# Third edge convolution of a fused graph network: the second norm is moved one and two quads behind the first, and TensorE adds the bias

## The chip, the cores and the metric

The kernel runs on one core of a Trainium2 chip. Its engines are PE (TensorE, matrix products into PSUM), PEld (TensorE's loading of weights), DVE (VectorE), ACT (ScalarE), POOL (GpSimd) and SP (SyncE, which issues most DMAs). The metric is the time of one execution in microseconds (us); the median of several executions is compared.

## What is computed

Four small graph networks follow each other: two GCN convolutions, two SAGE convolutions, three edge convolutions and four attention layers, with a layer norm and an addition of earlier features between the networks. Each has 25,000 edges over 50,000 nodes of 128 features. The change lies in the edge convolutions. For layer l of three:

```python
hx = h @ lin_w[l]
ea = relu(edge_attr @ edge_w1[l] + edge_b1[l]) @ edge_w2[l] + edge_b2[l]
msg = hx[row] * w[:, None] + ea
out = segment_sum(msg, col, num_segments=n) + bias[l]
mu = out.mean(-1, keepdims=True)
var = ((out - mu) ** 2).mean(-1, keepdims=True)
h = relu((out - mu) * rsqrt(var + LN_EPS) * ln_w[l] + ln_b[l])
```

After the third layer h is added to an earlier x, and the sum is normed again (the "second norm" here), cut at zero and multiplied with the first attention layer's weights.

## The kernel before

The edges are sorted by target node, cut into 196 tiles of 128 and worked through in 49 quads of four tiles (512 rows), from the last to the first. `KINDS` gives the twelve stages that run one after the other: X, C1, C2, S1, S2, LA, LA, LB, GA, GA, GA, GZ. LA is an edge convolution with its norm, LB the third one with both norms. POOL starts a stage's gathers (line 864) when the whole output of the stage before is stored. Every engine then runs its own program, two quads per turn of its loop, and waits for the others by semaphores; `Steps` counts the named steps (vd: DVE's, ad and ad_t: ACT's, pd: PE's).

In quad n of LA and LB:

- PE (`tile`) sums the messages of quad n+1, tiles 3 to 0: `FS` and `S` are 0/1 selection matrices that DVE writes (`select`, for quad n+2), `CR` and `LO` carry rows over the borders of tiles. `edge_hidden` (eat, ew) and `edge_terms` (ones_row and ew with H1T) make the edge terms of quad n+2; `edge_relu` on ACT lies between them. In LB, `edge_terms` stands at tile 2 and `tail_turn` (transposition of GN) behind it. The sums of a quad lie in PSUM bank 0 or 2.
- DVE adds the bias while it copies the sums into U (line 1349, step "comb"), takes mean and variance (`sums`: BATCH_NORM_STATS2 and AGGREGATE) and the factors (`coef`: rs and nb, from ACT's square root sd), and makes the messages of quad n+2 (line 1264), which need `edge_terms`.
- ACT scales (`scaled`) into GN in LA and into U in LB.
- In LB, `finish_lb` follows on DVE in the same quad: lnw, lnb, x (with XIN, the earlier features), second stats, aggr, rs and nb; ACT scales RB into GN. Only the rest of the tail is behind by one quad (`BEHIND`): PE turns GN (`tail_turn`), ACT copies it to OT, PE multiplies it with WX (`tail_rows`), and ACT copies the rows to RO and NV.
- In LA, PE multiplies OT with linw between the tiles of the next quad (`late_rows`), and ACT writes RO and then OT.

So every quad of LB runs through both norms on DVE before DVE takes up the next. The call that does it:

```python
                    finish(s, kind, n, h, ahead, turn)
                    if more and kind in ("LA", "LB"):
                        messages(s, n + 2, h)
                    if kind == "LB":
                        finish_lb(s, n)
```

Of the kernel before, what the change touches and what calls it, by code (L numbers as in the profile page):

```python
# [21 lines left out]
P = 128  # L22
N = 50000
E = 25000
D = 128
# [3 lines left out]
QUADS = T // 4  # L29
# [14 lines left out]
FIRSTS = CARRY_ROW[3] + 1  # L44
ONE_BANK = ('C1', 'C2', 'S1', 'S2', 'LA', 'LB')
# [51 lines left out]
def gnn_program(nc, a, out):  # L97
# [4 lines left out]
    with ctx:  # L102
# [22 lines left out]
        ones_row = sb("ones_row", [P, P], bf16)  # L125
# [16 lines left out]
        bias_r = sb("bias_r", [P, 3, D])  # L142
# [54 lines left out]
        den = sb("den", [P, 4, 2])  # L197
        ea_in = sb("ea_in", [P, 4, ED])
# [35 lines left out]
        b_in, b_rest, b_sum = (lend(2 * ROOM + 7600 + k * 384, 3, D)[0:3] for k in range(3))  # L234
        b_high, b_mid = (lend(2 * ROOM + 8800 + k * 192, 3, 64)[0:3].bitcast(bf16) for k in (0, 1))
# [3 lines left out]
        e_rest = lend(2 * ROOM + 9300 + 512, 2, 4 * ED)  # L239

# [63 lines left out]
        def steps(name, order, by=1, start=0):  # L304
# [21 lines left out]
            "LA": ("comb", "stats", "aggr", "rs", "nb"),  # L326
            "LB": ("comb", "stats", "aggr", "rs", "nb", "lnw", "lnb", "x", "stats2", "aggr2", "rs2", "nb2"),
# [12 lines left out]
        BEHIND = ("S2", "LB")  # L340
# [101 lines left out]
        loads += [(bias_r[:, l, :], a["L2_gnn_bias"][l].partition_broadcast(P)) for l in range(3)]  # L442
        loads += [(w_in[ED * k:ED * k + ED, :, :], a["L2_gnn_edge_w1"].rearrange("l p c -> p l c")) for k in range(8)]
        loads += [(b_in[:, l, :], a["L2_gnn_edge_b2"][l].partition_broadcast(3)) for l in range(3)]
# [120 lines left out]
        def _(sp):  # L565
# [101 lines left out]
            for s, kind in STAGES[1:]:  # L667
# [10 lines left out]
                def load(n):  # L678
# [7 lines left out]
                    if kind in xin.order:  # L686
                        sp.wait_ge(vd.sem, vd.at(s, n) if first else vd.last(s, n, "x"))
                        sp.dma_start(XIN[:, :, :], quad_rows(X_SRC[s], quad(n))).then_inc(xin.sem, 16)

                def store_x(n):  # L690
                    xstep = {"C2": "x", "S2": "x", "LB": "x"}.get(kind)
                    if xstep:
                        sp.wait_ge(vd.sem, vd.at(s, n, xstep))
                        sp.dma_start(quad_rows(X_DST[s], quad(n)), RB[:, :, :]).then_inc(st_x.sem, 16)
# [13 lines left out]
                if kind == "GZ":  # L708
                    load(0)
                    with sp.Fori(0, LAST) as n:  # L710
                        load(n + 1)
                else:
                    behind = kind in BEHIND + LATE

# [24 lines left out]
        def _(pool):  # L739
# [5 lines left out]
            g.memset(ones_row[:, :], 1.0).then_inc(c_pool, 1)  # L745
            pool.wait_ge(c_pool, 4)
            g.affine_select(out=ident[:, :], in_=ident[:, :], compare_op=ALU.not_equal, fill=1.0, base=0,
# [175 lines left out]
        def _(dve):  # L923
# [79 lines left out]
            for in_, rest, sum_, high, mid, mask, to in (  # L1003
                    (w_in, w_rest, w_sum, w_high, w_mid, is_part, ew1[:, :, :]),
                    (b_in, b_rest, b_sum, b_high, b_mid, ident[0:3, 0:3], None)):
# [18 lines left out]
            link(v.tensor_scalar(c2_r[:, :], bias_r[:, 2, :], mv[:, 0, 0:1], rs[:, 0:1], ALU.subtract, ALU.mult))  # L1024
# [207 lines left out]
            def select(s, n, h, j):  # L1232
# [16 lines left out]
                to = S[:, 4 * h + j, :]  # L1249
                if weight is None:  # L1250
# [42 lines left out]
            def finish(s, kind, n, h, ahead, turn=0):  # L1293
# [90 lines left out]
            def finish_lb(s, n):  # L1384

                dve.wait_ge(ad.sem, ad.at(s, n, "n"))
# [694 lines left out]
```

## Time and profile before

| | |
|---|---|
| median of 3 runs | 6893.03 us (6882.67 to 6896.57) |
| the profiled execution: its time | 6876.37 us |
| its span, first to last instruction | 6874.6 us |
| mean granted TensorE clock | 0.840 of 2.4 GHz |
| busy share: PE, PEld, DVE, ACT, POOL | 66%, 55%, 56%, 43%, 52% |
| stages LA, LA, LB (first to last line 1349) | 3486 to 3767, 3790 to 4070, 4094 to 4632 us |

The shares are means over twelve stages that run one after the other; what a change in one stage does is read from that stage's own rows.

### The profile page before, as it was taken

The numbers are of one execution on the slowest core, as the hardware profiler recorded it, in microseconds if no ns is written. First come the engines' busy times: TensorE is split into PE (matmuls) and PEld (weight loads), VectorE is DVE, ScalarE is ACT, GpSimd is POOL, SyncE is SP. The second block draws the span as 40 slices with busy tenths as digits, with TensorE's granted clock in tenths as the row PEclk, the third lists the DMA queues.
The fourth block names the chain that finished last, engine by engine and source line by source line (L and its number), as shares of the span: only waits on it lengthen the run. The fifth ranks groups of instructions, "written<-read, shape, count | busy, mean of one in ns | idle before, by whom it ended". The sixth has DMA issues, their size and how long they took to land. (4 is left out here: it accounts for less than half of the span.)

```text
span 6874.6 us, 127291 instructions
## 1 busy us (share of the span) xinstructions
PE 4515.9 (66%) x28875; PEld 3780.7 (55%) x28950; DVE 3833.9 (56%) x13851; ACT 2953.7 (43%) x7261; POOL 3552.3 (52%) x4582
## 2 busy tenths in 40 slices
PE   4888888888878767887789986660281282183065
PEld 2666666666656666666778876660271172072064
DVE  5666666766654487335777777770360261162176
ACT  3666666666633233334567765550130031031043
POOL 3434343444457174714655757106556556656666
PEclk9899999999999966998899998875695596596566
DMA  2555444445444275535743334322232132132133
GB/s 81 158 162 160 164 166 165 163 171 173 163 127 116 80 202 166 141 103 157 216 122 101 114 99 134 93 81 55 55 105 62 49 104 69 44 104 76 46 109 91
DMA packets 1002697, 815.63 MB, mean 119 GB/s; under 512 B 103820, under 2 KB 836818, under 8 KB 1002616
## 3 DMA queue, kind: packets, MB, share of 16 engines
q1 hardware_dynamic: 908536, 650.27, 30.8%
q0 software_dynamic: 94080, 164.48, 9.3%
q8 instruction: 26, 0.43, 0.0%
q14 instruction: 55, 0.45, 0.0%
HBM read 359.28 MB, written 459.01 MB: 119 GB/s over the span
## 5 line engine op out<-in xcount | busy, mean ns | idle before, releaser
L864 POOL DMA_INDIRECT G<-table,idx_all x1568 | 1525.4, 973 | 1284.9 <-issue 669.2
L1435 PE MATMUL PS<-G,S 128*128 (+2 forms) x4312 | 857.6, 306 | 5.8 <-DMA G<-table,idx_all 1.7
L1435 PEld LDWEIGHTS PS<-G,S 128*128 128x128 f32 x4312 | 733.8, 221 | 56.5 <-issue 48.1
L864 POOL DMA_INDIRECT G<-table,idx_l x588 | 583.2, 992 | 338.7 <-issue 178.3
L1758 ACT ACTIVATE CR<-PS 65x128 f32<-65x128 f32 (+3 forms) x1078 | 289.2, 268 | 1017.2 <-PE PS L1435 1005.6
L1435 PE MATMUL PS<-CR,LO 97*128 97x128 f32 (+1 forms) x4312 | 658.7, 302 | 64.6 <-ACT CR L1758 64.6
L1432 PE MATMUL PS<-ident,ES 128*98 128x128 f32 x16 | 4.2, 421 | 1003.5 <-DVE ES L475 1003.5
L1435 PE MATMUL PS<-G,FS 128*65 (+2 forms) x3234 | 514.2, 299 | 215.0 <-DVE den L1367 100.6
L1435 PEld LDWEIGHTS PS<-CR,LO 97*128 97x128 f32 x4312 | 610.8, 218 | 77.3 <-ACT CR L1758 77.3
L475 DVE COPY ES<-G 128x392 f32<-128x392 f32 x4 | 2.1, 527 | 1018.0 <-DMA G<-table,idx_all 1018.0
L1432 PEld LDWEIGHTS PS<-ident,ES 128*98 128x98 f32 x16 | 2.6, 191 | 1004.7 <-issue 1004.6
L1435 PEld LDWEIGHTS PS<-G,FS 128*65 128x65 f32 x3234 | 391.4, 150 | 278.9 <-issue 256.2
L1435 PE MATMUL PS<-w,H1T 128*128 128x128 f32 x2352 | 358.5, 311 | 224.8 <-DVE H1T L1099 193.8
L1758 ACT ACTIVATE G<-G 128x128 f32<-128x128 f32 x1176 | 483.0, 482 | 13.9 <-DVE G L1085 0.6
L1758 ACT ACTIVATE W<-V 98x1024 f32<-98x1024 f32 x4 | 4.2, 1056 | 1093.1 <-DVE V L517 1093.1
L1435 PEld LDWEIGHTS PS<-w,H1T 128*128 128x128 f32 x2352 | 325.9, 219 | 252.1 <-issue 214.7
L1138 DVE COPY G<-PS 128x520 f32<-128x520 f32 x392 | 271.2, 692 | 281.9 <-DMA table<-G 179.5
L1240 DVE TENSOR_TENSOR LO<-iota_row,relK 128x512 f32<-128x512 f32 x539 | 406.4, 754 | 0.1
L1251 DVE TENSOR_SCALAR S<-iota_row,rel 128x128 f32<-128x128 f32 x1372 | 380.7, 281 | 0.4 <-PE PS L1435 0.4
L1435 PEld LDWEIGHTS PS<-WX,G 128*128 128x128 f32 x2352 | 290.4, 191 | 160.2 <-issue 160.1
L886 POOL TENSOR_TENSOR OWN<-OWN,PT 128x256 f32<-128x256 f32 x294 | 175.7, 619 | 325.0 <-DMA OWN<-table 325.0
L1435 PE MATMUL PS<-WX,G 128*128 128x130 f32 x2352 | 321.6, 280 | 27.5 <-DVE G L1138 23.6
(292 smaller groups left out, 11284.0 us busy)
## 6 DMA issues: line engine op xcount, KB each, us to landing
table<-G SPq DMA_DIRECT2D x392, 260.0 KB, 2.7
table<-G SPq DMA_DIRECT2D x392, 256.0 KB, 2.6
table<-RO SPq DMA_DIRECT2D x245, 256.0 KB
table<-RO SPq DMA_DIRECT2D x196, 260.0 KB
OWN<-table SPq DMA_DIRECT2D x196, 260.0 KB
XIN<-xrows SPq DMA_DIRECT2D x196, 256.0 KB
OWN<-table SPq DMA_DIRECT2D x147, 256.0 KB
xrows<-RB SPq DMA_DIRECT2D x147, 256.0 KB
```

The costliest lines, as they stand in the source:

```text
L475: v.tensor_copy(ES[:, :, :], G[:, :, D:GW].rearrange("p t h -> p h t")).then_inc(m_v.sem, 1)
L864: g.indirect_dma_start(G[:, t, 0:w], None, TAB[s], bass.IndirectOffsetOnAxis(ap=idx[:, t:t + 1], axis=0)).then_inc(gat[t % 4].sem, 16)
L886: last = g.tensor_tensor(oh, oh, wide(PT[:, 2 + h, ds(Q4, 4)], 64), ALU.mult)
L1138: done(q, 3, v.tensor_copy(PR[t], pair(6)))
L1240: v.tensor_tensor(LO[:, 4 * h:4 * h + 4, :], iota_row[:, :].unsqueeze(1).to_broadcast([P, 4, P]), wide(relK[:, ds(Q4, 4)], P), ALU.is_equal)
L1251: i = v.tensor_scalar(to, iota_row[:, :], rel[:, ds(Q4 + j, 1)], None, ALU.is_equal)
L1432: return nc.tensor.transpose(o, i, ident[0:k, 0:k])
L1435: return nc.tensor.matmul(o, l, r, start=start, stop=stop)
L1758: return nc.scalar.activation(o, i, fn, **kw)
```

## The change

In LA and LB, TensorE adds the bias: one bf16 matrix product (`ones_bias` with `eb2`, whose rows 32 to 34 now hold the bias in three bf16 pieces) opens the PSUM bank of each quad, `ones_row` is masked to the rows below 32, and the prologue cuts the bias as it did the edge bias. DVE takes its stats from PSUM and ACT scales from PSUM, so the addition of line 1349 is gone; the bank is free again when ACT has scaled ("n"), where before it was free after "comb".

In LB the first norm of quad n now runs with lnw, lnb, x and the second stats of quad n-1, and with the second factors and second scaling of quad n-2. The second norm has its own stat2, mv2, sd2, rs2 and nb2 and its own counts (vd2, vd3, ad2), and the scaled rows alternate between U and OWN (`LBU`). The four selections S of a quad are one instruction. On PE all four tiles of quad n+1 come first, then `tail_turn` of n-2, then `edge_terms` of n+2, then `tail_rows` of n-2. DVE runs two more turns at the end. The other stages keep their order; PE's and ACT's loops start at quad 3 everywhere, with quads 1 and 2 written out.

The core of the diff:

```diff
+        LBU = (U[:, :, :], OWN[:, :, 0:D])
...
+        vd2 = steps("vd2", {"LB": ("lnw", "lnb", "x", "stats", "aggr")})
+        vd3 = steps("vd3", {"LB": ("rs", "nb")})
+        ad2 = steps("ad2", {"LB": ("sd", "g")})
+        BEHIND = {"S2": 1, "LB": 2}
...
+        loads += [(b_in[BIAS:BIAS + 3, l, :], a["L2_gnn_bias"][l].partition_broadcast(3)) for l in range(3)]
...
+                elif kind == "LB":
+
+                    def turn(n):
+                        at = n if isinstance(n, int) else 2
+                        if at < LAST - 2:
+                            load_attr(n + 3)
+                        if at > 0:
+                            load(n)
+                            store_x(n - 1)
+                        if at > 1:
+                            store(n - 2)
...
+            for in_, rest, sum_, high, mid, mask, to, row in (
+                    (w_in, w_rest, w_sum, w_high, w_mid, is_part, ew1[:, :, :], 0),
+                    *[(b_in[r:r + 3], b_rest[r:r + 3], b_sum[r:r + 3], b_high[r:r + 3], b_mid[r:r + 3],
+                       ident[r:r + 3, r:r + 3], None, r) for r in (0, BIAS)]):
...
+                if KINDS[s] == "LB":
+                    if j == 2:
+                        v.tensor_tensor(S[:, 4 * h:4 * h + 4, :], iota_row[:, :].unsqueeze(1).to_broadcast([P, 4, P]),
+                                        wide(rel[:, ds(Q4, 4)], P), ALU.is_equal).then_inc(sel.sem, 4)
+                    return
...
-                elif kind in ("LA", "LB"):
-                    if kind == "LA":
-                        dve.wait_ge(ad.sem, ad.last(s, n, "n"))
+                elif kind == "LA":
                     aggregated(s, n)
-                    step(s, n, v.tensor_tensor(U4, A, on4(bias_r[:, s - 5, :]), ALU.add), "comb", s3)
-                    sums(s, n, U, "", (s2,), (s1,))
+                    sums(s, n, A, "", (s3, s2), (s1,))
                     coef(s, n, "", (s0,))
...
+            def finish_lb(s, n, h, ahead):
+
+                s3, s2, s1, s0 = ahead
+                x_, sums_ = LBU[1 - h], bank(2 * h)
+                now = not isinstance(n, int) or n <= LAST
+                late = not isinstance(n, int) or 0 < n <= LAST + 1
+                later = not isinstance(n, int) or n > 1
+                if now:
+                    aggregated(s, n)
+                    for j in range(4):
+                        i = v.bn_stats(stat[:, j, :], sums_[:, j, :])
+                    i.then_inc(vd.sem, 1)
+                if later:
+                    dve.wait_ge(ad2.sem, ad2.at(s, n - 2, "sd"))
+                    v.reciprocal(rs2[:, :], sd2[:, :]).then_inc(vd3.sem, 1)
+                if late:
+                    dve.wait_ge(ad.sem, ad.at(s, n - 1, "n"))
+                    lnw = step2(s, n - 1, v.tensor_tensor(x_, x_, on4(lnw_r[:, :]), ALU.mult), "lnw")
+                if later:
+                    alone(dve, (vd3.sem, vd3.at(s, n - 2, "rs")))
+                    v.scalar_tensor_tensor(nb2[:, :], mv2[:, :, 0], -1.0, rs2[:, :], ALU.mult,
+                                           ALU.mult).then_inc(vd3.sem, 1)
+                if now:
+                    alone(dve, (vd.sem, vd.at(s, n, "stats")))
+                    for j in range(4):
+                        i = v.bn_aggr(mv[:, j, :], stat[:, j, :])
+                    i.then_inc(vd.sem, 1)
+                s3()
+                if late:
+                    lnw()
+                    lnb = step2(s, n - 1, v.tensor_tensor(x_, x_, on4(lnb_r[:, :]), ALU.add), "lnb")
+                if now:
+                    dve.wait_ge(ad.sem, ad.at(s, n, "sd"))
+                    v.reciprocal(rs[:, :], sd[:, :]).then_inc(vd.sem, 1)
+                s2()
+                if now:
+                    alone(dve, (vd.sem, vd.at(s, n, "rs")))
+                    v.scalar_tensor_tensor(nb[:, :], mv[:, :, 0], -1.0, rs[:, :], ALU.mult, ALU.mult).then_inc(vd.sem, 1)
+                if late:
+                    dve.wait_ge(xin.sem, xin.at(s, n - 1, "rows"))
+                    dve.wait_ge(st_x.sem, st_x.at(s, n - 1))
+                    dve.wait_ge(ad2.sem, ad2.last(s, n - 1, "g"))
+                    lnb()
+                    x_made = step2(s, n - 1, v.scalar_tensor_tensor(RB[:, :, :], x_, 0.0, XIN[:, :, :],
+                                                                    ALU.max, ALU.add), "x")
+                if not isinstance(n, int) or n < LAST - 1:
+                    messages(s, n + 2, h)
+                if late:
+                    x_made()
+                    for j in range(4):
+                        i = v.bn_stats(stat2[:, j, :], RB[:, j, :])
+                    step2(s, n - 1, i, "stats")()
+                    for j in range(4):
+                        i = v.bn_aggr(mv2[:, j, :], stat2[:, j, :])
+                    i.then_inc(vd2.sem, 1)
...
-                    pe.wait_ge(vd.sem, vd.at(s, n, "comb") - 2 * len(vd.order[kind]))
+                    if kind in ("LA", "LB"):
+                        pe.wait_ge(ad.sem, ad.at(s, n, "n") - 2 * len(ad.order[kind]))
+                        mm(PS[:, 2 * h, :], ones_bias[:, :], eb2[:, s - 5, :, :].rearrange("p j c -> p (j c)"),
+                           True, False)
+                    else:
+                        pe.wait_ge(vd.sem, vd.at(s, n, "comb") - 2 * len(vd.order[kind]))
...
-                            if j == (2 if kind == "LB" else 1) and edge and at < LAST - 1:
+                            if j == (0 if kind == "LB" else 2) and at >= behind:
+                                tail_turn(s, n - behind)
+                            if j == (0 if kind == "LB" else 1) and edge and at < LAST - 1:
                                 edge_terms(s, n + 2)
-                            if j == 2 and kind in BEHIND and at:
-                                tail_turn(s, n - 1)
-                            if j == 0 and kind in BEHIND and at:
-                                tail_rows(s, n - 1)
+                            if j == 0 and at >= behind:
+                                tail_rows(s, n - behind)
...
-                    scaled(s, n, ACT.Identity, "", U)
+                    scaled(s, n, ACT.Identity, bank(2 * h))
...
                 elif kind == "LB":
-                    ahead(3)
+                    at = n if isinstance(n, int) else 2
+                    if at < LAST:
+                        carried(s, n + 1, 1 - h, 3)
                     sqrts(s, n)
-                    scaled(s, n, ACT.Identity, "", U, U)
-                    ahead(2, 1, 0)
-                    sqrts(s, n, "2")
-                    scaled(s, n, ACT.Relu, "2")
+                    if at > 1:
+                        scaled2(s, n - 2)
+                    if at < LAST - 1:
+                        edge_relu(s, n + 2)
+                    if at > 1:
+                        tail_turned(s, n - 2)
+                    scaled(s, n, ACT.Identity, bank(2 * h), LBU[h])
+                    if at < LAST:
+                        carried(s, n + 1, 1 - h, 0)
+                    if at:
+                        sqrts2(s, n - 1)
+                    if at > 1:
+                        tail_out(s, n - 2)
```

`step2` issues a step counted in vd2 and returns its wait; `sqrts2` and `scaled2` are ACT's square root and scaling with the second set of buffers.

Where instructions stand now, in LB. DVE (waits in brackets; G<-G,wl,PS are the messages), the last part of a quad behind the loop, before:

```order
L1264 SCALAR_TENSOR_TENSOR G<-G,wl,PS 128x128 [waits gat3,pd_e]
L1264 SCALAR_TENSOR_TENSOR G<-G,wl,PS 128x128 [waits gat2]
L1264 SCALAR_TENSOR_TENSOR G<-G,wl,PS 128x128 [waits gat1]
L1264 SCALAR_TENSOR_TENSOR G<-G,wl,PS 128x128 [waits gat0]
L1387 TENSOR_TENSOR U<-U,lnw_r 128x512 [waits ad]
L1388 TENSOR_TENSOR U<-U,lnb_r 128x512 [waits vd,c_pool]
L1392 SCALAR_TENSOR_TENSOR RB<-U,XIN 128x512 [waits st_x,xin,ad,vd,c_pool]
L1276 BN_STATS stat<-RB 128x6 [waits vd,c_pool]
L1276 BN_STATS stat<-RB 128x6 x3
L1279 BN_AGGR mv<-stat 128x2 [waits vd,c_pool]
L1279 BN_AGGR mv<-stat 128x2 x3
L1286 RECIPROCAL rs<-sd 128x4 [waits ad]
```

and after:

```order
L1465 RECIPROCAL rs<-sd 128x4 [waits ad]
L1293 TENSOR_TENSOR S<-iota_row,rel 128x512 [waits agg]
L1469 SCALAR_TENSOR_TENSOR nb<-mv,rs 128x4 [waits vd,c_pool]
L1475 SCALAR_TENSOR_TENSOR RB<-OWN,XIN 128x512 [waits c_pool,ad2,vd2,st_x,xin]
L1310 SCALAR_TENSOR_TENSOR G<-G,wl,PS 128x128 [waits gat3,pd_e]
L1310 SCALAR_TENSOR_TENSOR G<-G,wl,PS 128x128 [waits gat2]
L1310 SCALAR_TENSOR_TENSOR G<-G,wl,PS 128x128 [waits gat1]
L1310 SCALAR_TENSOR_TENSOR G<-G,wl,PS 128x128 [waits gat0]
L1482 BN_STATS stat<-RB 128x6 [waits vd2,c_pool]
L1482 BN_STATS stat<-RB 128x6 x3
L1485 BN_AGGR mv<-stat 128x2 [waits vd2,c_pool]
L1485 BN_AGGR mv<-stat 128x2 x3
```

x (RB<-) stands ahead of the messages, of the quad before; rs and nb of the second norm are no longer at the end.

ACT, one quad ahead of the loop, before:

```order
L1758 ACTIVATE CR<-PS 65x128 [waits rsum]
L1758 ACTIVATE CR<-PS 1x128 [waits agg]
L1758 ACTIVATE CR<-PS 65x128 [waits rsum]
L1758 ACTIVATE H1T<-PS,eb 128x512 [waits pd_e]
L1758 ACTIVATE sd<-mv,eps 128x4 [waits vd]
L1758 ACTIVATE U<-U,nb,rs 128x128 [waits vd]
L1758 ACTIVATE U<-U,nb,rs 128x128 x3
L1758 ACTIVATE CR<-PS 1x128 [waits agg]
L1758 ACTIVATE sd<-mv,eps 128x4 [waits vd]
L1758 ACTIVATE GN<-RB,nb,rs 128x128 [waits vd]
L1758 ACTIVATE GN<-RB,nb,rs 128x128 x3
```

and after:

```order
L1864 ACTIVATE CR<-PS 65x128 [waits rsum]
L1864 ACTIVATE sd<-mv,eps 128x4 [waits vd]
L1864 ACTIVATE GN<-RB,nb,rs 128x128 [waits vd3]
L1864 ACTIVATE GN<-RB,nb,rs 128x128 x3
L1864 ACTIVATE H1T<-PS,eb 128x512 [waits pd_e]
L1864 ACTIVATE OT<-PS 128x512 [waits pd]
L1864 ACTIVATE U<-PS,nb,rs 128x128 [waits vd]
L1864 ACTIVATE U<-PS,nb,rs 128x128 x3
L1864 ACTIVATE CR<-PS 1x128 [waits agg]
L1864 ACTIVATE sd<-mv,eps 128x4 [waits vd2]
L1864 ACTIVATE RO<-PS 128x520 [waits pd,st_t]
L1864 ACTIVATE NV<-PS 128x4x4
```

The scaling GN<-RB now stands ahead of H1T, and waits for vd3 of two quads before; sd of the first norm stands ahead of it.

PE, one quad ahead of the loop, before (PS<-eb,ones_row and PS<-ew,H1T are `edge_terms`):

```order
L1435 MATMUL PS<-G,FS 65x128 [waits mprod,sel,vd]
L1435 MATMUL PS<-G,FS 65x128 [waits mprod] x2
L1435 MATMUL PS<-G,S 128x128 [waits mprod]
L1435 MATMUL PS<-eat,ew 128x512 [waits eas]
L1435 MATMUL PS<-G,S 128x128 [waits mprod,sel]
L1435 MATMUL PS<-eb,ones_row 128x512 [waits mprod,ad_e]
L1435 MATMUL PS<-ew,H1T 128x128 x4
L1435 MATMUL PS<-G,S 128x128 [waits mprod,sel] x2
L1435 MATMUL PS<-CR,LO 128x128 [waits carry]
L1435 MATMUL PS<-CR,LO 128x128 x3
```

and after:

```order
L1531 MATMUL PS<-eb,ones_bias 128x512 [waits ad]
L1531 MATMUL PS<-G,FS 65x128 [waits mprod,sel]
L1531 MATMUL PS<-G,FS 65x128 [waits mprod] x2
L1531 MATMUL PS<-G,S 128x128 [waits mprod]
L1531 MATMUL PS<-eat,ew 128x512 [waits eas]
L1531 MATMUL PS<-G,S 128x128 [waits mprod,sel] x3
L1531 MATMUL PS<-CR,LO 128x128 [waits carry]
L1531 MATMUL PS<-CR,LO 128x128 x3
L1528 MATMUL PS<-ident,GN 128x128 [waits ad_t,ad2]
L1528 MATMUL PS<-ident,GN 128x128 x3
L1531 MATMUL PS<-eb,ones_row 128x512 [waits mprod,ad_e]
L1531 MATMUL PS<-ew,H1T 128x128 x4
```

The product with ones_bias is new, and `edge_terms` has moved from behind tile 3's sums to behind the transposition of GN.

## Rows read from the trace of the kernel before

**Rows 1.** Windows of LA and LB: busy us of PE, PEld, DVE, ACT, POOL; clock; DMA.
```profile
3500.00:3760.00 260.00, 250.05 (x1938) 225.42 (x1961) 204.15 (x941) 194.85 (x446) 174.33 (x176) 1.00 0.39 112
...
4100.00:4330.00 230.00, 143.61 (x871) 138.35 (x880) 168.10 (x697) 121.03 (x323) 176.29 (x176) 0.80 0.47 132
4345.00:4625.00 280.00, 177.01 (x1081) 170.63 (x1092) 202.34 (x840) 148.41 (x397) 0.00 (x0) 0.80 0.29 81
```

**Rows 2.** The bias addition of line 1349, in the first LA stage and in LB.
```profile
L1349 DVE TENSOR_TENSOR U<-PS,bias_r x49: 684/692/693, 3486.4 to 3766.6; 128x512 f32<-128x512 f32 x49
...
L1349 DVE TENSOR_TENSOR U<-PS,bias_r x49: 683/692/693, 4094.0 to 4632.2; 128x512 f32<-128x512 f32 x49
```

**Rows 3.** Timeline of one LB quad: start us, us, engine, line, operation, idle before.
```profile
4343.28 0.61 PE L1435 MATMUL PS<-eb,ones_row 128*128 128x512 bf16 x1 [4.73 <-ACT H1T L1758]
...
4343.68 1.92 PE L1435 MATMUL PS<-ew,H1T 128*128 128x128 f32 x8
...
4345.87 1.12 DVE L1264 SCALAR_TENSOR_TENSOR G<-G,wl,PS 128x128 f32 x4 [1.60 <-PE PS L1435]
...
4346.91 0.69 DVE L1387 TENSOR_TENSOR U<-U,lnw_r 128x512 f32<-128x512 f32 x1
...
4349.57 0.87 DVE L1276 BATCH_NORM_STATS2 stat<-RB 128x6 f32<-128x128 f32 x4
...
4350.55 0.38 DVE L1279 BATCH_NORM_AGGREGATE mv<-stat 128x2 f32<-128x6 f32 x4
...
4350.97 0.30 ACT L1758 ACTIVATE sd<-mv,eps 128x4 f32<-128x4 f32 x1 [1.77 <-DVE mv L1279]
...
4351.59 0.16 DVE L1287 SCALAR_TENSOR_TENSOR nb<-mv,rs 128x4 f32<-128x4 f32 x1
4351.78 1.65 ACT L1758 ACTIVATE GN<-RB,nb,rs 128x128 f32<-128x128 f32 x4 [0.52 <-DVE nb L1287]
4351.82 0.69 DVE L1349 TENSOR_TENSOR U<-PS,bias_r 128x512 f32<-128x512 f32 x1
...
4353.09 0.28 DVE L1251 TENSOR_SCALAR S<-iota_row,rel 128x128 f32<-128x128 f32 x1
```

**Rows 4.** Timeline of one quad of the first LA stage.
```profile
3706.01 0.39 PE L1435 MATMUL PS<-eb,ones_row 128*128 128x512 bf16 x1
...
3706.23 1.05 PE L1435 MATMUL PS<-ew,H1T 128*128 128x128 f32 x8
...
3707.56 1.12 DVE L1264 SCALAR_TENSOR_TENSOR G<-G,wl,PS 128x128 f32 x4 [0.78 <-PE PS L1435]
...
3708.51 0.65 PE L1432 MATMUL PS<-ident,GN 128*128 128x128 f32 x4
...
3708.95 0.60 ACT L1758 ACTIVATE RO<-PS 128x512 f32<-128x512 f32 x1
...
3709.44 0.77 ACT L1758 ACTIVATE OT<-PS,lnb_c,lnw_c 128x512 f32<-128x512 f32 x1
...
3710.27 0.49 PE L1435 MATMUL PS<-linw,OT 128*128 128x128 f32 x2 [0.23 <-ACT OT L1758]
...
3711.01 0.69 ACT L1758 ACTIVATE H1T<-PS,eb 128x512 f32<-128x512 f32 x1 [0.64 <-remote]
```

**Rows 5.** Who waited for OT in the first LA stage: us, times.
```profile
  PE PS L1435: 5.1, 23
```

**Rows 6.** Timeline of the prologue: DVE cuts the three-partition weights into pieces.
```profile
58.84 0.35 DVE L1006 CAST G<-G 3x384 bf16<-3x384 f32 x1
...
62.49 1.92 DVE L1017 CAST eb<-G 3x384 bf16<-3x384 f32 x4
```

**Rows 7.** Timeline of the end of LB and the start of the next stage.
```profile
4632.22 0.69 DVE L1349 TENSOR_TENSOR U<-PS,bias_r 128x512 f32<-128x512 f32 x1
...
4645.70 1.09 PE L1432 MATMUL PS<-ident,GN 128*128 128x128 f32 x4 [7.13 <-ACT NV L1758]
...
4653.31 0.95 POOL L864 DMA_INDIRECT G<-table,idx_all  x1 [314.59 <-DMA table<-RO]
```

More of the change, by code:

```diff
@@ L124, in gnn_program @@
         eps = sb("eps", [P, 1])
-        ones_row = sb("ones_row", [P, P], bf16)
+        ones_row, ones_bias = (sb(n, [P, P], bf16) for n in ("ones_row", "ones_bias"))
         w1 = sb("w1", [P, 256])
@@ L325, in gnn_program @@
             "S2": ("comb", "x", "stats", "aggr", "rs", "nb"),
-            "LA": ("comb", "stats", "aggr", "rs", "nb"),
-            "LB": ("comb", "stats", "aggr", "rs", "nb", "lnw", "lnb", "x", "stats2", "aggr2", "rs2", "nb2"),
+            "LA": ("stats", "aggr", "rs", "nb"),
+            "LB": ("stats", "aggr", "rs", "nb"),
             "GA": ("den", "comb", "dene", "rden", "norm"),
@@ L711, in _ @@
                         load(n + 1)
+                elif kind == "LB":
[8 more added lines that the diff above has]
+                            store(n - 2)
+                    for n in (0, 1, 2):
+                        load_attr(n)
+                    load(0)
+                    turn(0)
+                    turn(1)
+                    with sp.Fori(2, LAST - 2) as n:
+                        turn(n)
+                    for n in (LAST - 2, LAST - 1, LAST):
+                        turn(n)
+                    store_x(LAST)
+                    store(LAST - 1)
+                    store(LAST)
                 else:
-                    behind = kind in BEHIND + LATE
+                    behind = kind in BEHIND or kind in LATE
                     def turn(n):
@@ L1382, in finish, with step2 @@
                         v.tensor_tensor(OUTR[h][:, :, 0:D], U[:, :, :], XIN[:, :, :], ALU.add).then_inc(vd.sem, 1)
[L1384 to L1394 removed]
+            def step2(s, n, ins, name):
+                ins.then_inc(vd2.sem, 1)
+                return lambda: alone(dve, (vd2.sem, vd2.at(s, n, name)))
@@ L1733, in quad @@
                     if kind in BEHIND and at == LAST:
[L1734 to L1736 removed]
+                        tail_rows(s, n - behind)
+                        for k in range(n - behind + 1, n + 1):
+                            tail_turn(s, k)
+                            tail_rows(s, k)
                 if kind in ("LA", "LB"):
@@ L1747, in _ @@
                 quad(0, 0)
-                with pe.Fori(0, LAST // 2 - 1) as m:
+                quad(1, 1)
+                quad(2, 0)
+                with pe.Fori(1, LAST // 2 - 1) as m:
                     quad(m * 2 + 1, 1)
@@ L2049, in _ @@
                 quad(0, 0)
-                with act.Fori(0, LAST // 2 - 1) as m:
+                quad(1, 1)
+                quad(2, 0)
+                with act.Fori(1, LAST // 2 - 1) as m:
                     quad(m * 2 + 1, 1)
```

101 lines of the change are left out of this document (59 added, 42 removed), and 1 row of the table ad.

## The prediction

> **What bounds the kernel now.** I read the windows by stage first. In LA, PE is busy 250 of 260 us at the full granted clock; in LB no engine is: PE 177 of 280 us, DVE 202, ACT 148, at a mean clock of 0.80 [rows 1]. So LB is bound by a ring of waits. The bias addition stands once in each quad: its first and last start give periods of 280.2/48 = 5.84 us in LA and 538.2/48 = 11.21 us in LB [rows 2].
>
> The timeline of one LB quad shows the ring. DVE waits 1.60 us for the edge terms and makes the messages; then lnw, lnb, x, stats, aggr, ACT's square root, rs, nb, and ACT's scaling of 1.65 us. Only behind that scaling comes H1T on ACT, for which PE has then stood idle 4.73 us, and only then the edge terms of the next quad [rows 3]. POOL's gathers do not lengthen it: LB has them in its first part (176 of 230 us busy) and not in its second, and the DVE share (73% and 72%) and the clock are the same [rows 1].
>
> LA has another ring, of PE and ACT alone: the turned sums, RO, OT, PE's product of OT with linw, eat, H1T, edge terms, the border products, and again RO. PE waits for OT where that product starts (0.23 us in the quad shown), in 23 of 45 quads and 5.1 us in all [rows 4, 5].
>
> **LB, the new ring.** Durations at the upper of TensorE's two levels (2.4 GHz), counted from the start of the first stats of quad n:
>
> - DVE: stats 0.87, rs of n-2 taken as nb's 0.16, lnw 0.69, nb 0.16, aggr 0.38: 2.3 us [rows 3].
> - ACT: sd of n 0.30, then the second scaling of n-2, 1.65, which stands behind sd on ACT: 4.2 us [rows 3].
> - PE: the transposition 0.65: 4.9; H1T (0.69) runs beside it on ACT. Then `edge_terms`, from 3706.01 to 3707.28, 1.27: 6.15 us [rows 4].
> - DVE: 0.28 until the messages start (3707.28 to 3707.56), 1.04 until the next instruction can start (4345.87 to 4346.91): 7.5 us [rows 3, 4]. Before them DVE has LO, S, lnb, rs, nb and x to do, three 512-wide operations more of about 0.69 with LO, FS and the wide S; that ends at about 5.5, inside the wait. The bias addition and S in four parts (0.28 each) are gone from DVE, but this saves nothing here, since DVE waits for the edge terms anyway.
> - DVE: second stats to aggr 0.98, aggr 0.38, and 0.23 to the next quad (nb to the next addition) [rows 3]: 9.1 us.
>
> So T = 9.1 us with PE at its upper level. At the lower level (1.2 GHz) `edge_terms` took 4343.28 to 4345.60, 2.32 us, 1.05 more [rows 3], and the transposition 1.09, 0.44 more [rows 7]: T = 10.6. A mean clock of 0.80 means that four tenths of the time are at the lower level [rows 1]. I keep this share: PE still idles twice in a quad, about 2 us ahead of the transposition (border products done at about 2, scaling at 4.2) and some 0.5 us ahead of the border products. T = 9.1 + 0.4 x 1.5 = 9.7 us. LB then gains 48 x (11.21 - 9.7) = **72 us**.
>
> What leaves the path is covered: ACT's first scaling of n runs from about 5.5 to 7.1 and DVE wants it at 1.1 of the next quad, after 10 us; PE sums quad n+1 two thirds of a quad ahead of need. XIN is now loaded in SP's queue after x of the quad before (at 5.5) and wanted a whole period later; store_x and the table's store behind it on SP have the same room. Nothing on SP waits for something that is later than before by more than a quad.
>
> **Reading PSUM.** No row has stats or a scaled copy of 128 columns from PSUM. Below, nothing: the addition took 0.692 us from PSUM and lnw 0.69 from SBUF [rows 2, 3]. Above, for ACT: OT, scaled from PSUM, took 0.77 for 512 columns [rows 4]; four at that price are 3.1 instead of 1.65. In LB that is still off the ring; in LA the missing addition (0.69) covers half of the 1.4, and 0.7 x 96 = 67 us would be left. I take nothing, since the addition's row is nearest. For DVE the upper end is as much again per read, 0.87 more, 42 us in LB; I take nothing.
> The Trainium skill (VectorE: DVE Perf Modes, section on the TRN2 errata) speaks against this change: it gives VectorE a fixed 120 cycles for a source in PSUM and 58 in SBUF, ScalarE 172 and 224. Four stats would pay 0.26 us more on the ring, an estimate from that page, 12 us over LB; the sum would end at 6847 instead of 6835. The rows of the addition do not show it.
>
> **LA.** The new product is 512 columns in bf16. The one with ones_row holds PE for 0.22 us before the next starts (3706.01 to 3706.23) [rows 4]. It stands ahead of the wait for OT, which covers it in the 23 of 45 quads that wait 0.22 us on average [rows 5]. In the others nothing covers it but the register work of a loop turn. From both sides: 0, and 0.22 x 96 = 21 us. I take 0.15 in every second quad: **+7 us**. The addition that DVE loses is not in LA's ring, so LA gains nothing inside; its last quad, serial to the store, is 0.69 shorter in each of two stages: -1.4 us. The new wait for ACT's "n" costs nothing, since PE has already waited for the same scaling before it transposes. Behind it FS, S and eat are queued, for which H1T waits.
>
> **Prologue and drain.** DVE's cutting into pieces on three partitions runs serially from 58.84 to 64.41 [rows 6] and is now done twice: **+5.6 us**. From the last addition to the first gather of the next stage are 21.1 us [rows 7]. Now the second norm of the last two quads is left over, one after the other on ACT and PE: 1.65 + 1.09 + 0.7 for scaling, turning and copying once more, **+3.5 us** (bounds 0 and 7).
>
> **Sum.** -72 + 7 - 1.4 + 5.6 + 3.5 = -58 us. The profiled execution took 6876 and would take 6818; the median of the runs shown is 17 us higher, 6893, so the forecast is **6835 us**.
>
> **Rivals.**
> - The clock stays up. PE's idle piece falls from 4.73 us to about 2; the clock was at its full level through LA, where PE hardly idles [rows 1]. Then T = 9.1, gain 101, sum -86: 6807. For it: every idle piece is less than half as long. Against it: 2 us of 9 are still idle in one piece. Chance 0.27. The Trainium skill (TensorE: Matmul & The Clock Gate, "What's actually happening") has the clock fall when the array has been idle and return after sustained work; by it this rival's time holds.
> - The lower level falls on the ring each time, because the idle piece lies just ahead of the transposition and the edge terms: T = 10.6, gain 29, sum -14: 6879. For it: before, the edge terms behind the idle piece were at the lower level in the quad shown [rows 3]. Chance 0.17.
> - The ring is shorter than I think (the scaling on ACT gets ahead) and DVE alone bounds LB: its work by the same rows is about 7.9 us, with gaps 8.3. Gain 140: 6768. For it: DVE's idle is only 1 us a quad in my ring. Chance 0.06.
> - Slower. PE becomes LB's bound at the lower level: busy 0.63 x 11.2 = 7.1 us a quad at a clock of 0.80 is about 5.6 us of work at the upper one, with the bias 5.8, at the lower one 11.6. If the level stays low, T is 11.6 and more, +19 in LB and +15 elsewhere: 6927 or above. It decides from T = 10.9 on, where LB's gain equals the other terms. Against it: a PE that works without idling was at the full clock in LA [rows 1]. Chance 0.05.
>
> My forecast, T from 9.4 to 10.3, has 0.45. About 0.2% (14 us) is what a measurement can tell from no change. Faster by more: below 6879, all of the first and third rival, the forecast and half of the second: 0.86; within: 0.09; slower: 0.05. The range, 8 times in 10, goes from 6790 (the clock rival with an LA that costs nothing) to 6880 (the second rival).
>
> **What would show it.** Line 1442's stats should start every 9.7 us in LB; DVE should wait about 1 us for the edge terms ahead of the messages; `edge_terms` should start right behind the transposition of GN, and that right behind the scaling from RB; the clock in LB should be 0.80 or more. LA should keep 5.84 to 5.95 us with PE at the full clock. The prediction is wrong if the clock in LB differs much from 0.80, if scaling from PSUM takes much over 1.65 us, or if LA's period moves by more than 0.2 us.

## The result and the profile after

The changed kernel takes **6792.2 us** (median of 4 runs, 6787.6 to 6795.7); the kernel before, timed beside it, 6894.8 us (4 runs). The ratio is 0.9853, with a 95% interval of 0.9836 to 0.9870: some 102 us gained. In a later session it was 6789.6 against 6880.8, a ratio of 0.9864 (0.9848 to 0.9879), or 91 us. The changed kernel's two medians lie 3 us apart; the kernel before had medians of 6881 to 6882 in three later sessions (33 runs), 13 us under the first four runs, so 91 is the surer figure. The forecast was 6835 us, a gain of 58.

The stages show where it went. Each length runs from the first gather of a stage to that of the next; before and after were each profiled twice.

| us | to the first gather | S2 | LA, 1st | LA, 2nd | LB | three GA stages | whole span |
|---|---|---|---|---|---|---|---|
| before | 1970.7, 1971.4 | 316.6, 317.0 | 303.7, 302.4 | 303.9, 303.8 | 570.8, 572.4 | 1606.2, 1613.0 | 6874.6, 6883.6 |
| after | 1979.3, 1982.3 | 319.6, 317.8 | 300.1, 300.3 | 299.9, 300.4 | 470.7, 469.7 | 1619.1, 1615.1 | 6793.0, 6791.6 |

Stages left out differ by under 2 us. LB gives 101 us, the two LA stages 6, the beginning takes back 10, and the GA stages differ as much between two profiles of one kernel (7 us) as between the two kernels.

The windows of LA and LB after the change (columns as in [rows 1]):

```profile
3512.00:3772.00 260.00, 248.88 (x1960) 231.61 (x2004) 177.24 (x891) 181.11 (x446) 175.56 (x178) 1.00 0.40 112
...
4110.00:4330.00 220.00, 164.51 (x1040) 147.95 (x1062) 163.01 (x717) 133.53 (x376) 169.71 (x166) 0.87 0.54 148
4345.00:4530.00 185.00, 137.34 (x884) 123.12 (x901) 137.31 (x603) 115.13 (x325) 2.99 (x3) 0.88 0.37 102
```

LA is the same stage as before: PE is busy 249 of 260 us at the full clock. In LB PE is busy 75% of the time instead of 63%, and the clock rose from 0.80 to 0.87. The first statistics of LB, once a quad:

```profile
L1442 DVE BATCH_NORM_STATS2 stat<-PS x196: 266/281/300, 4099.6 to 4534.5; 128x6 f32<-128x128 f32 x196
```

The last quad's four begin at 4533.92 (below), so the period is 434.3/48 = **9.05 us**, where [rows 2] gave 11.21 and the forecast 9.7. One whole turn of the new ring, from the timeline of the changed kernel, with PE at its upper level:

```profile
4399.33 0.89 DVE L1442 BATCH_NORM_STATS2 stat<-PS 128x6 f32<-128x128 f32 x4
...
4400.22 0.66 DVE L1449 TENSOR_TENSOR U<-U,lnw_r 128x512 f32<-128x512 f32 x1
...
4400.87 0.38 DVE L1457 BATCH_NORM_AGGREGATE mv<-stat 128x2 f32<-128x6 f32 x4
...
4401.28 0.30 ACT L1864 ACTIVATE sd<-mv,eps 128x4 f32<-128x4 f32 x1 [0.82 <-DVE mv L1457]
4401.48 1.63 ACT L1864 ACTIVATE GN<-RB,nb,rs 128x128 f32<-128x128 f32 x4
...
4403.02 0.67 ACT L1864 ACTIVATE H1T<-PS,eb 128x512 f32<-128x512 f32 x1
...
4403.25 0.66 PE L1528 MATMUL PS<-ident,GN 128*128 128x128 f32 x4 [1.57 <-ACT GN L1864]
...
4403.82 0.39 PE L1531 MATMUL PS<-eb,ones_row 128*128 128x512 bf16 x1
...
4404.04 1.05 PE L1531 MATMUL PS<-ew,H1T 128*128 128x128 f32 x8
...
4404.44 1.50 ACT L1864 ACTIVATE OWN<-PS,nb,rs 128x128 f32<-128x128 f32 x4
...
4405.40 1.12 DVE L1310 SCALAR_TENSOR_TENSOR G<-G,wl,PS 128x128 f32 x4 [1.33 <-PE PS L1531]
...
4406.44 0.87 DVE L1482 BATCH_NORM_STATS2 stat<-RB 128x6 f32<-128x128 f32 x4
...
4407.41 0.38 DVE L1485 BATCH_NORM_AGGREGATE mv<-stat 128x2 f32<-128x6 f32 x4
...
4408.09 0.89 DVE L1442 BATCH_NORM_STATS2 stat<-PS 128x6 f32<-128x128 f32 x4 [0.30 <-issue]
```

The steps are those of the forecast: 8.76 us from 4399.33 to 4408.09. The [0.30] of issue in front of the last row comes in every second quad. In a kernel whose PE stays at the upper level (the filler run below) the statistics start 8.76 and 8.38 us apart in turn, so that I take 8.57 on average for this ring. The next quad of the same timeline has PE at its lower level. There the ring took until 4417.86, 9.77 us, for these rows:

```profile
4412.00 1.11 PE L1528 MATMUL PS<-ident,GN 128*128 128x128 f32 x4 [1.95 <-ACT GN L1864]
...
4413.33 1.91 PE L1531 MATMUL PS<-ew,H1T 128*128 128x128 f32 x8 [0.22 <-issue]
```

Who waits in 4110 to 4330 is in the groups (busy us, mean ns of one | idle before):

```profile
L1310 DVE SCALAR_TENSOR_TENSOR G<-G,wl,PS 128x128 f32 x92 | 25.8, 344 | 47.7 <-PE PS L1531 47.7
...
L1528 PE MATMUL PS<-ident,GN 128*128 128x128 f32 x96 | 18.6, 325 | 42.3 <-ACT GN L1864 42.3
```

That is 23 or 24 quads: DVE waits 2.0 us in each for the edge terms, and PE 1.8 us for the scaling. Before, PE's idle piece was 4.73 us, in front of the edge terms [rows 3]. The prologue and the end of LB, where the forecast had two small costs:

```profile
64.49 0.35 DVE L1047 CAST G<-G 3x384 bf16<-3x384 f32 x1
...
68.15 1.92 DVE L1058 CAST eb<-G 3x384 bf16<-3x384 f32 x4
70.11 0.29 DVE L1060 BATCH_NORM_STATS2 stat<-bias_r 128x6 f32<-128x128 f32 x1
...
4533.92 0.89 DVE L1442 BATCH_NORM_STATS2 stat<-PS 128x6 f32<-128x128 f32 x4 [1.25 <-ACT CR L1864]
...
4558.36 0.94 POOL L904 DMA_INDIRECT G<-table,idx_all  x1 [209.76 <-DMA table<-RO]
```

The second cut takes 70.11 - 64.49 = 5.6 us. From the last start to the next stage's gather are 24.4 us, where it was 21.1 [rows 7].

### The profile page after: what moved, and what is told of

Same layout as the page of the kernel before. It is cut to its first block and busy times, and to the rows that moved or that the text cites. A ratio compares the mean times of both kernels' runs of the same rounds, so it can differ in the third digit from the quotient of the medians.

```text
span 6793.0 us, 126255 instructions
## 1 busy us (share of the span) xinstructions
PE 4495.4 (66%) x28956; PEld 3757.9 (55%) x29097; DVE 3721.0 (55%) x13568; ACT 2906.8 (43%) x7261; POOL 3556.3 (52%) x4585
## 5 line engine op out<-in xcount | busy, mean ns | idle before, releaser
L1531 PE MATMUL PS<-G,S 128*128 (+2 forms) x4312 | 829.5, 300 | 5.1 <-DMA G<-table,idx_all 1.5
L1531 PEld LDWEIGHTS PS<-G,S 128*128 128x128 f32 x4312 | 710.0, 215 | 54.8 <-issue 46.8
L1531 PE MATMUL PS<-CR,LO 97*128 97x128 f32 (+1 forms) x4312 | 635.9, 295 | 83.7 <-ACT CR L1864 83.4
L1531 PEld LDWEIGHTS PS<-CR,LO 97*128 97x128 f32 x4312 | 581.9, 209 | 103.0 <-ACT CR L1864 103.0
```

The costliest lines, as they stand in the source:

```text
L1531: return nc.tensor.matmul(o, l, r, start=start, stop=stop)
```

## The experiments

The theory: LB's period is a ring that runs once round DVE, ACT and PE (first statistics, second scaling, transposition, edge terms, messages, second statistics); what lies on it costs in full, what lies in DVE's wait in front of the messages costs nothing, and PE's lower clock level costs about 0.6 us a quad. The rivals: DVE's own busy time sets the period; the gain is the missing addition and not the order; the clock can't be had back by the kernel. Each median is told beside the one of the kernel before in the same session: 6881.8 for the first four runs, 6881.8 for the next four, 6880.8 for the last four. Their spread makes differences under some 8 us between sessions mean little, so that the length of LB in the profile is given each time.

**The two halves of the change.** First TensorE's bias alone, in the kernel before:

```diff
-step(s, n, v.tensor_tensor(U4, A, on4(bias_r[:, s - 5, :]), ALU.add), "comb", s3)   # DVE, LA and LB
+mm(PS[:, 2 * h, :], ones_bias[:, :], eb2[:, s - 5, :, :].rearrange("p j c -> p (j c)"), True, False)   # PE
```

> The kernel before, with TensorE's bias in LA and LB and without the change of LB's order: the first and second norms of LB stay one behind the other as before. If nearly all of LB's gain (100 us) is the new order, this LB stays within 0.44+1.1 us a quad of the period before (11.2 us), that is gains 20 to 55 us by the addition of 0.7 to 1.1 us that no longer stands in the chain, and LA gives 4 us back as in the changed kernel: 6835 to 6870. If the prediction's 'gone from DVE saves nothing' holds, LB gains under 5 us: 6885 to 6892. If the GA stages' +4 us each (three stages, +13 in all) come with the bias constants and not with the order, they are here too; otherwise GA is as before.

Measured: 6881.9, a ratio of 0.9998 (0.9989 to 1.0007). LB 568.4, LA 298.9 and 299.9. The bias taken from DVE is worth 3 us in LB in the old order and 8 in the two LA stages; the beginning is 8 longer in this profile. The timeline of this kernel shows why it does nothing in LB:

```profile
4355.34 0.16 DVE L1295 SCALAR_TENSOR_TENSOR nb<-mv,rs 128x4 f32<-128x4 f32 x1
4355.53 1.65 ACT L1768 ACTIVATE GN<-RB,nb,rs 128x128 f32<-128x128 f32 x4 [0.52 <-DVE nb L1295]
4355.56 0.89 DVE L1284 BATCH_NORM_STATS2 stat<-PS 128x6 f32<-128x128 f32 x4
```

In the old order the next quad's first norm starts on DVE together with ACT's 1.65 us of scaling, as the addition did in [rows 3]; it is in that scaling's shadow. Then the new order alone, DVE adding in LA and LB:

```diff
+v.tensor_tensor(LBU[h], sums_, on4(bias_r[:, :]), ALU.add)      # ahead of the first statistics
-v.bn_stats(stat[:, j, :], sums_[:, j, :])
+v.bn_stats(stat[:, j, :], LBU[h][:, j, :])
```

> The other half of the change alone: LB in the new order with its own buffers, and DVE adding the bias in LA and in LB as before (in LB directly ahead of the first statistics, which then read the sum). If the chain statistics, second scaling, transposition, edge terms, messages sets the period, the addition and the wait for it stand in it: LB comes out near the 516 us of the run with one DVE operation more at that place, 510 to 530, LA at 304, the whole at 6835 to 6845. If the addition is as free in the new order as it was in the old one, LB is 471 to 475 and the whole 6790 to 6800.

Measured: 6833.1, ratio 0.9927 (0.9914 to 0.9941), LB 518.2, LA 303.9 and 301.9. From this kernel's timeline:

```profile
4407.75 0.38 DVE L1492 BATCH_NORM_AGGREGATE mv<-stat 128x2 f32<-128x6 f32 x4
4408.06 0.69 DVE L1445 TENSOR_TENSOR OWN<-PS,bias_r 128x512 f32<-128x512 f32 x1
...
4408.85 0.87 DVE L1452 BATCH_NORM_STATS2 stat<-OWN 128x6 f32<-128x128 f32 x4
```

Here the addition stands on the ring: 0.79 us from its start to that of the statistics. So LB is 571.6 before (mean of two), 568.4 with the bias alone, 518.2 with the order alone, 470.2 with both. The halves give 3 and 53 apart, and 101 together: the bias is worth 48 us behind the order, 1.0 us a quad. 0.79 of it is the ring; the rest goes with the clock, 0.83 and 0.84 in the two windows here and 0.87 and 0.88 with both halves.

**One DVE operation more, at two places of the changed kernel.**

```diff
+v.tensor_tensor(spare[:, :, :], sums_, on4(lnw_r[:, :]), ALU.add)             # a: ahead of the first statistics
+v.tensor_tensor(spare[:, :, :], on4(lnb_r[:, :]), on4(lnw_r[:, :]), ALU.add)  # b: ahead of the messages
```

> The changed kernel, with one DVE addition of 4x128 columns from PSUM more (its output isn't used), put directly ahead of the first statistics in LB, where before the bias addition stood. If the ring from statistics to messages and back sets the period, the 0.7 us comes in full each quad: 49 x 0.7 = +34, 6826 (a part may be given back by or lost to the clock: +25 to +50). If DVE's wait in front of the messages takes it up, +0 to 5: 6792 to 6797.

> The changed kernel, with the same kind of DVE addition of 4x128 columns more (from SBUF, its output isn't used), but directly ahead of LB's messages, where DVE waits 1.3 us or more for the edge terms. If the ring sets the period, the wait takes it up: 6792 to 6800. If DVE's busy time sets it, +0.7 x 49 = +34: 6826.

Measured, a: 6830.6, ratio 0.9919, LB 515.6: +45 us, 0.93 a quad. b: 6781.2, ratio 0.9856 (0.9841 to 0.9871), LB 472.1: +2. The waits of the messages in b:

```profile
L1311 DVE SCALAR_TENSOR_TENSOR G<-G,wl,PS 128x128 f32 x96 | 26.9, 343 | 34.5 <-PE PS L1534 33.8 <-DMA G<-table,idx_l 0.7
```

That is 1.44 us a quad, and 2.07 in the changed kernel (47.7 in 23 quads): the wait took in 0.6 of the operation's 0.68 us. The same kind of operation costs 45 us at one place and 2 at the other, 4.65 us further in the same quad (4401.47 and 4406.12 in b's timeline). That rules out DVE's busy time as the bound. In a the statistics start 0.61 us behind the operation (4405.03 and 4405.64); the rest of the 0.93 goes with the clock, which was 0.84 and 0.83 in the two windows.

**S in four parts**, as before the change:

```diff
-v.tensor_tensor(S[:, 4 * h:4 * h + 4, :], iota_row[:, :].unsqueeze(1).to_broadcast([P, 4, P]),
-                wide(rel[:, ds(Q4, 4)], P), ALU.is_equal)
+for k in (3, 2, 1, 0):
+    v.tensor_scalar(S[:, 4 * h + k, :], iota_row[:, :], rel[:, ds(Q4 + k, 1)], None, ALU.is_equal)
```

> The changed kernel, with LB's selections built by four instructions in place of one (0.44 us more of DVE a quad). In the changed LB, DVE waits 1.3 to 2.7 us in front of the messages, after S: if that wait absorbs it, the time stays at 6792 (within 5). If DVE's busy time sets the period, it rises by 0.44 x 49 = 21: 6813.

Measured: 6785.1, ratio 0.9854, LB 469.1. It costs nothing. The operation was smaller than I wrote: the four took 21.7 us in 24 quads and the one 15.8, 0.25 us a quad, so that a DVE bound would have cost 12 us and not 21.

**LA's bias by DVE**, the rest as changed:

> The changed kernel, with LA's bias added by DVE as before; LB is left as changed. If LA's -3.7 and -4.0 us are the added bias gone from the start and the end of each LA stage, both LA stages go back to 303.7: 6800, +8 against the changed kernel. If they are something else that the change brought, LA stays at 300 and the time at 6792.

Measured: LA 304.0 and 303.8, LB 470.6, whole 6789.1. By the profile LA's 4 us a stage are TensorE's bias (in nine kernels with it LA took 298.7 to 300.7, in those without 301.9 to 304.0); in the whole time 8 us are no more than the spread.

**The clock.** Six matmuls of 128 columns more in each quad, into a bank that nobody reads, ahead of the transposition:

```diff
 def tail_turn(s, n):
+    if KINDS[s] == "LB":
+        for j in range(6):
+            mm(PS[:, 3, 0:P], ident[:, :], iota_row[:, :])
```

> The changed kernel, with six matmuls of 128 columns more in each quad of LB, ahead of the transposition, into a bank that nobody reads (work that the result doesn't need). If the lower granted clock (0.87 to 0.88 in LB) comes from TensorE's waits and costs a quad at the lower level about 1 us in the ring, the granted clock goes to 1.0 and the period to 8.8: LB gains 15 to 25 us: 6767 to 6777. If the matmuls cost as much as they give: 6790 to 6810, clock higher. If the clock isn't theirs to hold, clock as before and 6792 or more.

Measured: 6749.7, ratio 0.9808 (0.9794 to 0.9821), LB 436.6, a larger gain than I expected. Its windows, its first statistics, and three of them in a row (the view ends behind the first instruction of the last):

```profile
4110.00:4330.00 220.00, 193.78 (x1465) 166.27 (x1464) 175.33 (x768) 146.74 (x412) 169.41 (x167) 1.00 0.56 156
4345.00:4490.00 145.00, 128.02 (x968) 109.82 (x967) 116.10 (x510) 96.19 (x273) 0.00 (x0) 1.00 0.38 107
...
L1442 DVE BATCH_NORM_STATS2 stat<-PS x196: 265/281/300, 4096.2 to 4500.8; 128x6 f32<-128x128 f32 x196
...
4382.84 0.89 DVE L1442 BATCH_NORM_STATS2 stat<-PS 128x6 f32<-128x128 f32 x4 [0.30 <-issue]
...
4391.21 0.89 DVE L1442 BATCH_NORM_STATS2 stat<-PS 128x6 f32<-128x128 f32 x4
...
4399.97 0.30 DVE L1442 BATCH_NORM_STATS2 stat<-PS 128x6 f32<-128x128 f32 x1 [0.30 <-issue]
```

PE idles less, the clock is full, and the period is 404.6/48 = 8.4 us (the row's last start is up to 0.6 behind the first of its four; from first to first it is 4500.23 - 4096.24, 8.42 us a quad) for 9.05. So the lower level cost the changed kernel 0.63 us in each quad, 30 us, and LB is 34 shorter in all: the end of the stage, from the last start to the next gather, is 3 shorter too (21.0 us for 24.4). This run answers the clock rival: with the clock up, T is 8.4 and not 9.1.

**The ring broken.** First PE does the edge terms ahead of the transposition; in the second kernel ACT also does the relu ahead of the square root and the scaling:

```diff
 # PE, at tile 0
-tail_turn(s, n - behind); edge_terms(s, n + 2)
+edge_terms(s, n + 2); tail_turn(s, n - behind)
 # ACT, second kernel only
-sqrts(s, n); scaled2(s, n - 2); edge_relu(s, n + 2)
+edge_relu(s, n + 2); sqrts(s, n); scaled2(s, n - 2)
```

> The changed kernel, with TensorE doing LB's edge terms of the next quad ahead of the transposition of the quad behind. If TensorE's order puts transposition (0.66 us) into the ring between the scaling and the edge terms, taking it out shortens each quad by up to 0.66 us less what else then comes last; the relu on ScalarE for those terms (behind the scaling there) still holds them, so the gain is 0 to 0.6 us a quad: 6763 to 6792, and I take 6775. If the ring goes another way than through the transposition, 6792.

> As the last, and ScalarE does the relu for the next quad's edge terms ahead of the square root and the scaling of the quad behind, so that the edge terms wait for neither. If the ring statistics, scaling, relu, edge terms, messages is what sets the period, it is broken here and DVE's own busy time (7.4 us a quad of the windows and some 0.7 of gaps) sets it: 8.0 to 8.3 us for 8.75 to 10, LB gains 35 to 60 us: 6732 to 6757. If the period is set by something else (TensorE at the lower clock, or the waits on transfers), 6780 to 6792.

Measured, the first: 6760.2, ratio 0.9820 (0.9807 to 0.9834), LB 448.8. The 21 us in LB lie in the 0 to 29 that I expected, and the reason was wrong. From its timeline:

```profile
4299.94 1.63 ACT L1866 ACTIVATE GN<-RB,nb,rs 128x128 f32<-128x128 f32 x4
...
4301.47 0.67 ACT L1866 ACTIVATE H1T<-PS,eb 128x512 f32<-128x512 f32 x1
...
4302.27 0.39 PE L1531 MATMUL PS<-eb,ones_row 128*128 128x512 bf16 x1 [1.78 <-ACT H1T L1866]
```

From the start of the scaling to the product with ones_row are 2.33 us; in the changed kernel they were 2.34 (4401.48 to 4403.82). At the upper level ACT's relu takes as long as PE's transposition beside it, so nothing came off the ring. What came is the clock: 0.96 and 0.98 in the two windows of LB, for 0.87 and 0.88, and the products with H1T take over 1.5 us in 2 of 49 quads, where in the changed kernel they did in 28.

The second: **6690.2, ratio 0.9719** (0.9706 to 0.9733), LB 382.0, the fastest kernel here, some 100 us under the changed one, 88 of them in LB. Its windows, its first statistics and three groups of 4110 to 4330:

```profile
4110.00:4330.00 220.00, 185.41 (x1356) 155.99 (x1355) 204.10 (x907) 175.48 (x483) 169.59 (x166) 0.99 0.64 176
4345.00:4430.00 85.00, 72.13 (x534) 60.89 (x532) 79.44 (x351) 68.82 (x188) 0.00 (x0) 1.00 0.44 124
...
L1442 DVE BATCH_NORM_STATS2 stat<-PS x196: 278/281/301, 4091.5 to 4438.1; 128x6 f32<-128x128 f32 x196
...
L1310 DVE SCALAR_TENSOR_TENSOR G<-G,wl,PS 128x128 f32 x120 | 33.4, 338 | 0.0
...
L1475 DVE SCALAR_TENSOR_TENSOR RB<-U,XIN 128x512 f32<-128x512 f32 x15 | 11.2, 747 | 5.8 <-ACT GN L1866 5.8
L1475 DVE SCALAR_TENSOR_TENSOR RB<-OWN,XIN 128x512 f32<-128x512 f32 x15 | 10.4, 693 | 2.2
```

The period is 7.2 us, and DVE is busy 93% of it. My 8.0 to 8.3 was too long because 7.4 us a quad of busy time was misread: DVE's windows in the changed kernel give 163.01 x 9.05/220 = 6.7, and here 204.10 x 7.2/220 = 6.7 again. The wait in front of the messages is gone; 8.0 us in 30 quads remain in front of x, which overwrites RB and waits until ACT's second scaling has read it. Whether DVE now is the bound was asked with S in four parts in this kernel:

> The kernel with relu and edge terms ahead of the second norm's scaling and transposition, with LB's selections built by four instructions in place of one (0.44 us more of DVE a quad). In the changed kernel the same edit cost nothing. If DVE's busy time is what sets LB's period now, it costs 0.44 x 49 = 21 us: 6711 against 6690. If another wait still sets it: 6690 to 6695.

Measured: 6691.6, ratio 0.9729, LB 383.2, +1 us. DVE was busy 4.4 us more in the window (208.49), and the idle time in front of x fell by 4.3:

```profile
L1476 DVE SCALAR_TENSOR_TENSOR RB<-U,XIN 128x512 f32<-128x512 f32 x15 | 10.5, 702 | 3.7 <-issue 2.6 <-ACT GN L1867 1.0
L1476 DVE SCALAR_TENSOR_TENSOR RB<-OWN,XIN 128x512 f32<-128x512 f32 x15 | 10.2, 680 | 0.0
```

The edit added little to DVE's work (the four selections took 27.5 us in 30 quads, the one 19.8, 0.26 a quad and not 0.44), and the wait in front of x took most of it. So the bound was not yet DVE alone, as I had expected; by these rows it is a second ring through RB and ACT's scaling that is about as long. No run shortened that ring, so that this is argued from the waits and not shown.

**Both kernels once more**, for the spread between executions:

> The kernel before, once more, for a second profile: whether the GA stages' 535 us and the first stage's 1971 us are its own (then 534 to 536 and 1970 to 1972 again, and the +4 and +9 of the changed kernel are the change's), or differ from one execution to the next by as much (then 535 to 540 and 1970 to 1980).

> The changed kernel once more, beside the two above on one chip: 6785 to 6795 and a ratio of 0.985 to 0.987; LB 470 to 472 us, LA 300. If the first stage and the GA stages vary between executions, this profile shows them elsewhere than 1979 and 540.

They are the second numbers of the table above. LB, LA and the time to the first gather came out within 3 us of the first profile; the GA stages of before did not (538.4, 537.8, 536.8 for 534.7, 535.7, 535.8), so no cost there can be put down to the change. The time to the first gather is less sure than two profiles make it look: ten more kernels with the second cut had 1970.4 to 1979.2, the lowest of them under that of the kernel before.

## Why the forecast was right in kind and short in size

- **What bounded LB**: right. A ring of waits, now shown by the same kind of operation costing 45 us on it and 2 us in its wait.
- **The steps of the new ring**: right, each in its place. Their sum at the upper level, 9.1 us, was too long; it measured 8.57. The step that failed is "stats 0.87, rs 0.16, lnw 0.69, nb 0.16", 1.88 us, which took 1.54 (4399.33 to 4400.87): the durations of rows were added, but each DVE instruction starts up to 0.1 us before the one ahead of it ends. sd to scaling was 0.20 for 0.30, the transposition 0.57 (4403.25 to 4403.82) for 0.65, the scaling to the transposition 1.77 for 1.65, and the way back to the next statistics 0.68 or 0.30 for 0.61; 0.06 is rounding upwards in the forecast's sum. Together 0.5 us a quad, 25 us. Starts should be subtracted, as the forecast did elsewhere.
- **The clock's term**, 0.4 x 1.5 = 0.6 us a quad: right in its product, measured 0.63 by the filler. Its parts were not: the clock rose to 0.87, so that a quarter of the time is at the lower level and not four tenths, but those stretches fall on PE's part of the ring more often than that: in the trace of the changed kernel the products with H1T take over 1.5 us in 28 of 49 quads (1.05 at the upper level) and the transposition over 0.9 in 16. So the second rival, by which the lower level falls on the ring each time, had part of the truth; its 10.6 us a quad did not come. The rival "the clock stays up" did not come true. Its 6807 is nearer to the result than 6835 only because it shares the ring that was too long; with the clock up, the result is 6750.
- **LB in sum**: the 48 periods gave 104 us for 72. Of the 32, 25 are the sum of the ring at the upper level, and some 7 are the first and last quads, which are shorter than the steady ones (8.42 us over all 48 periods of the filler run, 8.57 steady); the clock's 0.03 us more a quad takes 1 back. The stage as a whole gave 101, since its end is 3 us longer, which the forecast had as a term of its own.
- **"This saves nothing here"**, of the bias addition and of S in four parts: right for S (-1 us), wrong for the addition. DVE's wait absorbs only what stands between the statistics and the messages; the addition would stand ahead of the statistics, on the ring, for 48 us. The sum did not suffer, since its ring began at the statistics, but the reason given for the addition is wrong: DVE's wait could not have taken it in. That the bias alone gave 3 us in the old order has another cause, the shadow of ACT's scaling.
- **Reading PSUM**: priced at nothing, near enough. Four stats took 0.89 from PSUM and 0.87 from SBUF (0.89 against 0.87 in the rows above); ACT's scaling took 1.50 from PSUM (4404.44) and 1.63 from SBUF (4401.48). The Trainium skill (VectorE: DVE Perf Modes, section on the TRN2 errata), from whose cycles the forecast estimated 0.26 us more for four stats from PSUM, is not borne out: the rows differ by 0.02 us. For ScalarE, where it gives PSUM the lower cost, the rows agree in direction.
- **LA**: +7 - 1.4 was forecast, -6 to -7 came. The term of 0.15 us for the bias product in every second quad fails: the period in the middle of the stage is 5.83 us before and after, so the product is covered in all quads. The addition was gone from the start of the stage as well as from its end: the first statistics of the first LA stage start 11.5 us behind the first gather, for 13.0.
- **Prologue and drain**: 5.6 us as forecast, in each kernel; how much of it reaches the end is less sure (the stage's end scatters by 9 us). Drain 24.4 - 21.1 = 3.3 for 3.5.
- **The slower rival**, PE as LB's bound at the lower level: no trace of it. PE is busy 75% of the time. **The rival with DVE alone as the bound** did not come true either, since DVE waits 2.0 us a quad for the edge terms; its 8.3 us were too high besides, as the kernel with the ring broken runs at 7.2.
- **The signs it named**: the order of the instructions and LA's period are as it said. The clock in LB was 0.87 and not 0.80, and DVE's wait 2.0 us and not about 1 (1.33 with PE at its upper level).
- **The whole**: 58 forecast, 32 more from LB's periods and 12 more from LA make 102, the difference of the first medians. That this is also the first session's figure is partly luck: the two pairs of profiles are 82 and 92 us apart, because the beginning and the GA stages, which scatter by as much, took more back than the 5.6 us forecast.

## What to carry to other kernels

Draw the ring that sets the period, and price each edit by where it stands on it: an operation of 0.69 us cost 45 us at one place and 2 at another, and an edit that is worth nothing in one order (3 us) can be worth 48 once another edit has changed what it stands in. Two halves of a change can't be judged one at a time. Then look who waits in the ring for someone who merely stands ahead in a queue: moving the edge terms in front of a transposition, and their relu in front of a square root and a scaling, none of which they need, took 88 us more from LB, after 101 by the whole change. The first move alone gave 21, the relu behind it 67.

## What the runs showed of the hardware that was not expected

- Successive DVE instructions overlap in the rows: four statistics of 0.89 us, and the next instruction's start 0.81 us after theirs (4408.09, 4408.90 in the changed kernel's timeline). Adding the durations of the seven instructions in front of aggr (four statistics, rs, lnw, nb) made 0.34 us too much.
- Work that the result doesn't need made the kernel faster: six matmuls a quad that nobody reads, with the granted clock in LB at 1.00 where it was 0.87, and 34 us less. A reordering without extra work had as high a clock (0.99 and 1.00, PE busy 84%).
- LB's granted clock went from 0.80 to 0.87 when PE's idle piece fell from 4.73 us [rows 3] to 1.57 or 1.95. With the edge terms first the piece was still 1.78 us and the clock 0.96 and 0.98, with the same work in another order. So the longest idle piece alone does not say what will be granted; what does was not tried. That the clock falls after the array idles and comes back with sustained work (the Trainium skill, TensorE: Matmul & The Clock Gate, "What's actually happening") agrees with the filler run, in which PE is busy 88% of the time. That the clock stays up in the changed kernel, as the forecast took from the same section for its first rival, does not agree with the trace: the clock there was 0.87, and the measurement decides.
